# Routing weights of a mixture of experts spread by repeating DMAs instead of matmuls, with a second bank for U

## What is computed

```
x = x + 0.5 * _L0_ffn_ref(_layernorm(x), ...)      # mixture of experts + shared expert
x = x + _L0_attn_ref(_layernorm(x), ...)           # linear attention, 16 heads of 8
x = x + 0.5 * _L0_ffn_ref(_layernorm(x), ...)
x = x + 0.5 * _L1_ffn_ref(_layernorm(x), ...)      # MLP 128 -> 512 -> 128, relu
x = x + _L1_attn_ref(_layernorm(x), ...)
x = x + 0.5 * _L1_ffn_ref(_layernorm(x), ...)
```

```
scores = jax.nn.sigmoid(x @ gate_weight.T)
topk_w, topk_idx = jax.lax.top_k(scores, 2);  topk_w = topk_w / (topk_w.sum(-1) + 1e-20)
comb = zeros((T, 16)).at[rows, topk_idx].set(topk_w)
g = silu(einsum('th,ehi->eti', x, We_gate));  u = einsum('th,ehi->eti', x, We_up)
ye = einsum('eti,eih->eth', g * u, We_down);  y = einsum('te,eth->th', comb, ye)
shared = silu(x @ Ws_gate) * (x @ Ws_up) @ Ws_down
```

## Time and profile before

| | us |
|---|---|
| median of 3 runs (2250.55 to 2264.78) | 2261.32 |
| the profiled execution's own time | 2249.78 |
| its span, first to last instruction | 2248.0 |
| TensorE matmul busy | 1996.7 (89%) |
| VectorE busy | 1687.3 (75%) |
| ScalarE busy | 1083.7 (48%) |
| GpSimd busy | 585.0 (26%) |

### The profile page before, as it was taken

How to read it: one execution, slowest core, us unless ns; L and a number is a source line. 1 busy time by engine, 2 the same in 40 slices (tenths; PEclk the granted TensorE clock), 3 DMA queues, 4 the chain that set the end, 5 groups by cost and what they waited for, 6 DMA issues and landing times. The chain is left out here.

```text
span 2248.0 us, 34225 instructions
## 1 busy us (share of the span) xinstructions
PE 1996.7 (89%) x12660; PEld 1369.6 (61%) x12660; DVE 1687.3 (75%) x4160; ACT 1083.7 (48%) x1907; POOL 585.0 (26%) x621
## 2 busy tenths in 40 slices
PE   3998989898999899889989758999999999999997
PEld 3787778777877787777877623444444444444443
DVE  5767776767766776767677449888888888888882
ACT  3333323333333333333333117777777777777774
POOL 2331332223222323233313031222222222222211
PEclk9999999999999999999999959999999999999999
DMA  3000000000000000000000032222222222222220
GB/s 117 6 10 10 1 10 10 10 1 10 10 10 5 6 10 10 10 1 10 10 6 1 10 98 71 76 76 76 76 75 76 76 76 76 76 76 79 70 69 10
DMA packets 47941, 85.28 MB, mean 38 GB/s; under 512 B 5728, under 2 KB 9056, under 8 KB 47712
## 3 DMA queue, kind: packets, MB, share of 16 engines
q1 hardware_dynamic: 45872, 81.32, 11.4%
q10 hardware_dynamic: 1904, 1.78, 0.2%
HBM read 49.26 MB, written 34.87 MB: 37 GB/s over the span
## 5 line engine op out<-in xcount | busy, mean ns | idle before, releaser
L1263 DVE TENSOR_REDUCE b_nm<-b_MX 128x1 f32<-128x512 f32 x1024 | 647.6, 682 | 74.1 <-PE b_MX L1379 66.8
L1163 ACT ACTIVATE b_pr<-b_ST 128x512 f32<-128x512 f32 x1024 | 550.8, 601 | 163.1 <-PE b_ST L1366 161.9
L1379 PE MATMUL b_MX<-b_kt,b_qt 32*128 32x512 f32 x1024 | 353.9, 511 | 43.0 <-DMA b_qt<-staging 10.1
L383 ACT ACTIVATE s<-G 128x512 f32<-128x512 f32 x306 | 182.9, 598 | 432.7 <-PE G L685 423.7
L690 PE MATMUL Y<-w_wd,h 128*128 128x128 f32 x2448 | 335.3, 281 | 8.6 <-DVE h L544 7.9
L690 PEld LDWEIGHTS Y<-w_wd,h 128*128 128x128 f32 x2448 | 315.4, 195 | 24.0 <-DVE h L544 13.3
L535 DVE TENSOR_TENSOR su<-U,s 128x512 f32<-128x512 f32 x272 | 186.1, 684 | 161.3 <-ACT s L383 83.3
L1366 PEld LDWEIGHTS b_ST<-b_qm,b_kt 32*128 32x128 f32 x1024 | 119.1, 185 | 304.6 <-ACT b_pr L1163 190.8
L1366 PE MATMUL b_ST<-b_qm,b_kt 32*128 32x512 f32 x1024 | 293.6, 503 | 10.8 <-ACT b_pr L1163 10.7
L1394 PE MATMUL b_PV<-b_pr,b_va 128*32 128x512 f32 x2048 | 280.5, 620 | 0.0
L544 DVE TENSOR_TENSOR h<-C,su 128x512 f32<-128x512 f32 x272 | 188.1, 691 | 9.3
(11 more groups left out here) (237 smaller groups left out, 3497.3 us busy)
## 6 DMA issues: line engine op xcount, KB each, us to landing
b_kt<-staging SPq DMA_DIRECT2D x64, 256.0 KB, 2.9
b_qt<-staging SPq DMA_DIRECT2D x64, 256.0 KB, 3.4
staging<-b_khi SPq DMA_DIRECT2D x32, 256.0 KB, 3.0
staging<-b_qhi SPq DMA_DIRECT2D x32, 256.0 KB, 3.0
xin<-in_x SPq DMA_DIRECT2D x17, 256.0 KB, 2.6
mid<-xo SPq DMA_DIRECT2D x17, 256.0 KB, 2.0
b_x<-mid SPq DMA_DIRECT2D x16, 256.0 KB, 2.9
staging<-b_klo SPq DMA_DIRECT2D x16, 256.0 KB, 3.0
```

What stands on the lines that cost most here:

```text
L383: nc.scalar.activation(sbuf_s[n % 2][:], G[n % 2][:], ACT.Silu).then_inc(act_done.sem, 1)
L1163: nc.scalar.activation(pr[k % 2][:, j], bank[:].rearrange("p a b -> p (a b)"), ACT.Exp, scale=SM_SCALE).then_inc(used["st"].sem, 1)
L1263: nc.vector.tensor_reduce(nm[g % 2][:, t, c:c + 1], bank[:].rearrange("p a b -> p (a b)"), AX.X, ALU.max).then_inc(used["mx"].sem, 1)
L1379: pe.matmul(flat(MX[place % MX_BANKS]), qt[g][rows_of(j), u // HG % T], flat(kt_[g])[rows_of(j)], start=True, stop=True).then_inc(made["mx ...
```

## The change

The weights no longer go through TensorE. `comb` is kept as it is, without halves, and transposed during the preparation (one step behind `weights`) instead of at step 0. ScalarE copies its 16 rows to `cT`. SP writes them to a DRAM tensor `spread` and then reads them back with four DMAs whose source repeats each row over 64 partitions, into `cw` [128 x 8 x 512]. `w_pairs` goes, bank C becomes a second bank of U. VectorE computes `su = U * cw` and then `h = su * s`. `s` has three buffers. The preparation in attention slots stands at the steps of the MLP slots. `weigh` (GpSimd) is there, but its table is empty and nothing is issued.

```diff
 PREPARE = {
     MLP: {"statistics": 0, "transpose": 2, "low": 2, "logits": 3, "first": 4, "second": 5, "weights": 6},
-    ATT: {"statistics": 1, "transpose": 3, "low": 4, "logits": 5, "first": 6, "second": 7, "weights": 8},
+    ATT: {"statistics": 0, "transpose": 2, "low": 2, "logits": 3, "first": 4, "second": 5, "weights": 6},
 }
+WEIGHED_BY_POOL = {MLP: (), ATT: ()}
...
-        U = ps("U", [P, T, P])
-        C = ps("C", [P, T, P])
+        U = [ps(f"U{k}", [P, T, P]) for k in range(2)]
...
+            def spread_weights(q, i):
+                k = number(q, i)
+                p = k % 2
+                sp.wait_ge(cT_ready.sem, cT_ready.at(i, q + 1))
+                if k >= 2:
+                    sp.wait_ge(spread[p], spread_until(k - 2))
+                sp.dma_start(spread_dram[p], cT[p][:].rearrange("e t p -> e (t p)")).then_inc(rows_out, 16)
+                if k >= 2:
+                    sp.wait_ge(h_ready.sem, NT * (k - 1))
+                sp.wait_ge(rows_out, 16 * (k + 1))
+                for n in (0, TE // 2):
+                    for e in range(2):
+                        sp.dma_start(cw[p][e * I_E:(e + 1) * I_E, n:n + TE // 2].rearrange("p n t q -> p n (t q)"),
+                                     spread_dram[p].rearrange("(n two) q -> two n q", two=2)[e:e + 1, n:n + TE // 2]
+                                     .broadcast_to([I_E, TE // 2, N])).then_inc(spread[p], 16)
...
+            def weight_rows(q, i):
+                k = number(q, i)
+                act.wait_ge(combT_ready.sem, combT_ready.at(i, q + 1))
+                if k >= 2:
+                    act.wait_ge(rows_out, 16 * (k - 1))
+                nc.scalar.activation(cT[k % 2][:], Z[0:E], ACT.Copy).then_inc(cT_ready.sem, 1)
...
-                step(nc.vector.tensor_tensor(comb[:], first[:], share[:], ALU.mult))
-                own.settle()
-                step(nc.vector.tensor_copy(combh[:], comb[:]))
-                own.settle()
-                step(nc.vector.tensor_copy(comb2[:, :, 0:E], combh[:]))
-                nc.vector.tensor_tensor(comb2[:, :, E:2 * E], comb[:], combh[:],
-                                        ALU.subtract).then_inc(comb_ready.sem, 1)
+                wait_for(dve, combT_ready, i, q)
+                nc.vector.tensor_tensor(comb[:, :, 0:E], first[:], share[:], ALU.mult).then_inc(comb_ready.sem, 1)
...
-                nc.vector.tensor_tensor(out[:], U[:], sbuf_s[n % 2][:], ALU.mult).then_inc(up_used.sem, 1)
-            def routed(m, n, i):
-                nc.vector.tensor_tensor(h[n % 3][:], C[:], su[n % 2][:], ALU.mult).then_inc(h_ready.sem, 1)
+                    dve.wait_ge(spread[k % 2], spread_until(k))
+                    wait_for(dve, h_ready, i, g0 + n - 1)
+                    step(nc.vector.tensor_tensor(su[n % 2][:], U[n % 2][:], cw[k % 2][:, n - 1], ALU.mult))
+                    dve.wait_ge(act_done.sem, act_done.at(i, g0 + n + 1))
+                    own.settle()
+                    ins = nc.vector.tensor_tensor(out[:], su[n % 2][:], s[:], ALU.mult)
...
-                pe.matmul(flat(C), w["pairs"][:, n - 1], flat(cT[m % 2]), start=True,
-                          stop=True).then_inc(weight_ready.sem, 1)
...
-                    if n >= 1:
-                        pe.wait_ge(up_used.sem, up_used.at(i, g0 + n))
-                    product(U, w["wuh"][:, n], w["wul"][:, n], high, low).then_inc(up_ready.sem, 1)
-                    if n == 0:
-                        comb_transposes(m, i)
-                    else:
-                        routing_weights(m, n, i)
+                    if n >= 2:
+                        pe.wait_ge(h_ready.sem, h_ready.at(i, g0 + n - 1))
+                    product(U[n % 2], w["wuh"][:, n], w["wul"][:, n], high, low).then_inc(up_ready.sem, 1)
+                    if prepare and n == steps["weights"] + 1:
+                        comb_transposes(m + 1, i)
...
             main_transposes(-1, 0)
             logits(-1, 0)
+            comb_transposes(-1, 0)
             slot(-1, 0, None, True)
```

More of the change, by code:

```diff
@@ L153, in build_front @@
         den = sb("den", [P, T, 1])
[L154 to L159, removed]
+        comb = sb("comb", [P, T, P])
+        cT = [sb(f"cT{p}", [E, T, P]) for p in range(2)]
+        cw = [sb(f"cw{p}", [P, TE, T, P]) for p in range(2)]
+        sbuf_s = [sb(f"s{p}", [P, T, P]) for p in range(3)]
         su = [sb(f"su{k}", [P, T, P]) for k in range(2)]
@@ L243, in build_front @@
         oT_ready = sig("oT_ready", N_ATT)
+        spread = [ctx.enter_context(nc.semaphore(f"spread{p}")) for p in range(2)]
+        rows_out = ctx.enter_context(nc.semaphore("rows_out"))
+        weighed = ctx.enter_context(nc.semaphore("weighed"))
         comb_cleared = ctx.enter_context(nc.semaphore("comb_cleared"))
@@ L250, in build_front, with number, weighed_by_pool, weighed_until @@
         block = ctx.enter_context(nc.Block())
+        slots = NM * turns + 2
+        def number(m, i):
+            return NM * i + m + 1
+        def weighed_by_pool(s):
+            m = s - 1
+            return WEIGHED_BY_POOL[SIDE[m % NM] if 0 < s < slots - 1 else MLP]
+        def weighed_until(s, n):
+            return sum(len(weighed_by_pool(k)) for k in range(s)) + sum(1 for k in weighed_by_pool(s) if k <= n)
+        def spread_until(s):
+            return 16 * 4 * (s // 2 + 1)
+        def wait_for(eng, signal, i, n):
+            if signal.at(i, n) > 0:
+                eng.wait_ge(signal.sem, signal.at(i, n))
         def source(q):
@@ L275, in load @@
                 sp.dma_start(xin[p][:], xd[batch]).then_inc(x_loaded[p].sem, 16)
-            load(0, -1, 2)
[L278 to L290, removed]
+            def spread_weights(q, i):
[13 more added lines that the diff above has]
+                                     .broadcast_to([I_E, TE // 2, N])).then_inc(spread[p], 16)
+            spread_weights(-1, 0)
+            spread_weights(0, 0)
+            load(0, -1, 2)
+            for i in range(turns):
+                for m in range(NM):
+                    spread_weights(m + 1, i)
+                    if m % 2 == 1:
+                        store(i, m)
+                        if i < turns - 1:
+                            load(i, m, min(i * 2 + 3 + m // 2, 2 * turns - 1 - m // 2))
             sp.wait_ge(side_done.sem, side_done.at(turns, 1))
@@ L316, in main_normalise, with weigh @@
                 nc.gpsimd.tensor_tensor(z[:], z[:], rstd[:].broadcast_to([P, T, D]), ALU.mult).then_inc(z_ready.sem, 1)
+            def weigh(m, i, ns):
+                k = number(m, i)
+                for n in ns:
+                    if n in weighed_by_pool(k):
+                        pool.wait_ge(act_done.sem, act_done.at(i, NT * m + n + 1))
+                        pool.wait_ge(spread[k % 2], spread_until(k))
+                        s = sbuf_s[n % 3]
+                        nc.gpsimd.tensor_tensor(s[:], s[:], cw[k % 2][:, n - 1], ALU.mult).then_inc(weighed, 1)
             def side_start(m, i, k):
@@ L326, in _ @@
             main_normalise(0, 0)
+            weigh(-1, 0, range(1, NT))
             for i in range(turns):
@@ L330, in _ @@
                     main_normalise(m + 1, i)
+                    if SIDE[m] == MLP:
+                        weigh(m, i, range(1, NT))
                     if SIDE[m] == ATT:
                         a = nth(m)
+                        weigh(m, i, range(1, 4))
                         pool.wait_ge(ka_ready.sem, ka_ready.at(i, a + 1))
@@ L350, in _ @@
                         nc.gpsimd.tensor_tensor(og[:], og[:], ub[:], ALU.add).then_inc(og_ready.sem, 1)
+                        weigh(m, i, range(6, NT))
+            weigh(0, turns, range(1, NT))
             side_start(1, turns, 0)
@@ L408, in slot @@
                             scores(m + 1, i)
+                        if n == steps["weights"] + 1:
+                            weight_rows(m + 1, i)
             main_high(-1, 0)
@@ L1453, in build_weights @@
     sb("router", [P, 2 * E], F32R)
-    sb("pairs", [P, TE, P], F32R)
     for name, shape in parts.items():
@@ L1472, in build_weights @@
         router = scratch("router", [P, E])
-        pairs = scratch("pairs", [P, TE, P])
         theta_t = scratch("theta_t", [P, T, P])
@@ L1566, in _ @@
             wait_loads(dve, "others")
-            nc.vector.tensor_copy(w["pairs"][:], pairs[:])
             low_parts(dve, nc.vector, range(first_dve, len(halves)))
@@ L1662 @@
             w = build_weights(nc, front, back, args)
-            build_front(nc, w, args["x"], mid, args["c_ident"], NB // 2)
+            build_front(nc, w, args["x"], mid, args["c_ident"], spread, NB // 2)
         build_back(nc, w, mid, out, staging, args["c_tail"], NB)
```

64 lines of the change are left out of this document (25 added, 39 removed).

## The result

The changed kernel takes 2453.9 us (2452.8 to 2455.7, four runs), the one before 2256.4 us beside it: ratio 1.087, 95% interval 1.083 to 1.092. That is +197 us, where +35 was forecast: the sign was right, the size more than five times the forecast and outside the range. The profiled execution took 2454.8 us (span 2453.0). The back takes 958 us against 952, so the front has all but about 6 us of it. There TensorE's share fell from 91% to 81%, and its clock from 0.99 to 0.91.

A forecast was written before the change was run, and what follows sets the result against it. TensorE, busy 91% of the front, was taken to set the pace. Attention slots +38, MLP slots -9, start +7, setup -1 gave +35 us: 2285 profiled, 2297 on the median's scale; 8 in 10 range 2224 to 2375.

The forecast's parts named there:

- The transfers: Writing cT and four loads per slot: weights there 10.6 us after cT, needed at 11.0 to 11.4, counted as 0.
- The third rival: Weight loads from DRAM: repeated rows load slowly; half rate +200, 2497, chance 0.05; quarter lower +53, 2350, chance 0.12.
- a new wait of 3.2 us: Attention slot, step 4: TensorE waits before attend, as routing_first, ahead of mask_heads, meets GpSimd's block; 3.2 us.
- 2.8 us of new wait: Attention slot, before comb's transposes: comb ready at about 34.6 us, TensorE there at 31.8.
- The meetings: Attention slot: h and four of routing_first's instructions on VectorE each wait out one of GpSimd's.
- The slot: Attention slot: 40.6 us against 38.3, +2.4 us times 16, +38 us in all.
- The MLP slot: MLP slot, 35.2 us before: 0.5 us saved, times 17 slots, -9 us (ends -14 and +2).
- my far end: Attention slots: two waits of about 3 us each also lower TensorE's clock, up to +26 us more.
- The start: First slot: su of step 1 waits for the transfers until about 54.3 us, +7 us; setup loses the pairs, -1.
- C's matmuls: 272 matmuls on TensorE go, 0.23 us each, 63 us in all, of which not all shows.

## Why the prediction was wrong

- *The transfers, the step that failed.* "so 2.1 MB take 6.7 us", "the weights are there 10.6 us after cT", "I count 0". The 312 GB/s were read from loads to 128 partitions and applied to loads to 64. Against the 8.3 us from issue to landing stand 12.8 (751.55 to 764.36). The rate explains 2.8 of the 4.5 (9.5 less 6.7), or 3.5 at 205 GB/s; the rest is start and landing, which I had put at 1.6 without a row for it. The write took 1.6, not 2.1. So su was late by 3.35 us, and TensorE, as I had said, stood behind it on xls. The path was right, the rate wrong. By my own rule, each microsecond in all 33 slots, that is 110 us, and the runs with and without loads differ by 121; that these are so near is in part luck. From 120 to 1380 us su waited for a transfer in 25 slots only, 68.6 us together. The attention slots behind the first grew over the run without loads by 5.0 us (47.4 against 42.4), more than the wait, the MLP slots by 1.9 (37.2 against 35.3), less than it, and the last slot by 8.4. The third rival priced 1.6 us late at 2350 and 6.1 at 2497, and the result lies between them; but the two had a chance of 0.17, as I looked only at the repetition, which costs nothing.
- *The rest was too small as well:* by the profiled executions, 2331.6 without loads against 2249.8, it is +82 us and not +35 (+73 by the ratio), 47 more. What there is to say of it:
  - The waits. "a new wait of 3.2 us", "2.8 us of new wait": 2.5 and 2.5. The meetings came as named: kc 1.82, qc 1.72, en 1.26 and hit 1.19 instead of 0.2, comb 1.25, h 1.05 and 1.11. Undoing the order removed the one wait, as it should. Of routing_first's instructions only en and hit waited out one of GpSimd's in full, not four.
  - The slot. Forecast 40.6 us; without loads it is about 41.48 in 4 of the 15 attention slots behind the first and 42.69 in the others. The MLP slot, forecast 34.7 (35.2 less 0.5), takes 34.46 in one half of the cases and 36.08 in the other. What separates the two kinds is the clock, in this order of attention, MLP, and then the MLP and attention slots of the other kind:

```profile
549.94:592.63 42.69, 35.04 (x206) 30.31 (x205) 32.36 (x83) 11.91 (x19) 16.67 (x16) 0.92 0.02 7
592.63:628.71 36.08, 31.89 (x191) 27.49 (x190) 23.08 (x64) 12.86 (x20) 5.75 (x7) 0.95 0.02 9
...
750.17:784.63 34.46, 30.22 (x191) 25.99 (x190) 23.07 (x63) 12.86 (x20) 5.75 (x7) 1.00 0.02 9
784.63:826.11 41.48, 33.29 (x206) 28.99 (x205) 32.28 (x83) 11.91 (x19) 16.67 (x16) 0.96 0.03 7
```

  - The clock had been my far end, "up to +26 more", and I took none of it into the sum. It belonged there: the waits that I forecast myself were as long as the 2.4 us one behind which it fell before. The work in the MLP slots of the two kinds is the same and their difference is 1.6 us. The means, 42.4 and 35.3, are 4.1 and 0.1 above the kernel before, where I had +2.4 and -0.5: 25 and 10 us of the missing 47.
  - The start: without loads the first residual comes at 82.0 us, 69.0 before: +13, not the +6 of "+7 - 1", 7 more. The first attention slot, which still has its own loads, takes 46.9 us, 39.0 before: 5.5 more than forecast. (With half of the bytes it is 41.3.)
- *C's matmuls.* "Not all of it shows" was right: with the old order and no transfers 32 slots gain 31 us, about half. The 8 us of that whole run are these less the 24 that its first two slots pay for their own transfers; the back, which nobody changed, differs by up to 10 us between the profiled executions (952 to 962).
- *Not shown:* how the late loads' 121 us divide into the wait itself and the lower clock behind it. Only both together were taken away. TensorE's waits for xls, 120 to 1380 us, are 109 us with the loads and 30 without, so some 79 of the 121 are in them.

## What to carry to other kernels

Read a transfer's rate off rows that reach the same partitions, not only with rows of the same length; if one tile is filled in parts, let each part reach across all partitions, as every second one does, which here cost nothing in bytes and gave back 112 of 197 us. A transfer whose landing is "just in time" must be priced at its slowest plausible rate, since its lateness is paid once per slot. Work taken off the busiest engine pays only where no wait for another engine closes the gap, and a wait that you forecast can bring a lower clock with it: put that into the sum. A variant that drops work in all but its first slots has to be read by its later slots, not by its whole time.

## What the runs showed of the hardware

- Loads of 512 KB into 64 neighbouring partitions ran at 220 GB/s, with every DMA engine shown busy; into all 128, at 354; into every second one a packet took 90 ns, against 140 and 87. A busy share of 1.0 is no proof of full rate. Two queues with a half each didn't help (2447.8 against 2453.9 us).
- Repeating one row over 64 partitions costs no more than reading different rows (140 and 142 ns a packet).
- Instructions of VectorE with SBUF operands alone that started inside one of GpSimd's were held: of 64 columns, en, hit and comb ended within 0.1 us behind it (1.26, 1.19 and 1.25 instead of 0.2 us); h, of 512, ended 0.5 us behind it (1.05 and 1.11 instead of 0.69). This was foreseen for h without a row. A reduction with one operand (L540, at 780.64) was not held: 0.22 us.
